# One core: the products of a gated state-space mixer written as eight term rows, all summed by TensorE's accumulating transposes, and the router's logits taken from a padded gate chunk

## The chip, the core and the metric

One core of one Trainium2 chip. Time is device microseconds for one execution of the whole program. The kernel before was run three times: 261.28, 262.47 and 263.16 us, median 262.47. TensorE is called PE in the rows, VectorE DVE, ScalarE ACT, GpSimd POOL and the DMA queue's own engine SP.

## The reference

Two residual layers over x of shape (16, 128, 256), all float32. The first is a mixer, the second a mixture of experts:

```python
# mixer: k = v = ctx (16, 128, 256) as 16 heads of 8 channels; q = layernorm(x)
kv  = einsum('bhil,bhjl->bijhl', k_, v_)              # products of channels in a head
y   = irfft(rfft(kv, 2L) * rfft(ssm_kernel, 2L))[..., :L]   # causal convolution, per head
out = y + kv * D                                       # skip
out = einsum('bijhl,bhil->bjhl', out, q_)              # sum over i
x   = x + tanh(g_xattn) * out
# experts: 2048 tokens of 256, E = 8 experts of capacity 256, hidden 352
xt = layernorm(x);  probs = softmax(xt @ Wg);  e = argmax(probs)
out = W2[e](silu(xt W1[e]) * (xt W3[e])) * gate, dropped past the capacity
shared = silu(xt @ sw1) * (xt @ sw3) @ sw2             # for every token
x = x + tanh(g_ffn) * (out + shared)
```

## The kernel before, in words

**Mixer.** The 16 batches go in 4 groups of 4. A group has 8 units of 2 heads. Time is cut in 2 blocks of 128; a causal convolution is then a matmul with a Toeplitz matrix (`toep`, the skip D added to it on VectorE by `add_skip`, L868 to L873). kv is symmetric in i and j, so a head has 36 planes of products. They are made a quarter of a group (4 heads) at a time by GpSimd (`kv_products`) and ScalarE (`squares`), for the next group while the present one runs. For a unit (`convolve`, L923) TensorE does per head one matmul of 144 and one of 288 columns into the PSUM buffer z[s % 2]. VectorE (`products`, `multiply`, L360 to L378) multiplies the 36 planes by q in five instructions, 1,024 elements a partition, into a buffer `prod` of eight term rows. GpSimd (`add_halves`, L503) adds rows 0 to 3 and 4 to 7 into four rows of `half`. When all 8 units of a group are done, `turn_r` (L956) transposes the four rows of each block and sums them in PSUM: 4 accumulating transposes for each of 8 blocks, 32 in all, in two parts k = 0 and 1. VectorE adds the result to x (`first_residual`).

**Norms and router.** Layernorm takes `norm_stats` on VectorE, `scale_and_bias` on GpSimd, `normalise` on ScalarE (`norm1` for q, `norm2` for the tokens), and a turn on TensorE (`turn_q`, `turn_xT`). Tokens and gate/up weights are split in a high and a low part (fp32r), and three products stand for one; `weights_high` (ScalarE) and `weights_low` (VectorE) split the weights, `xT_high` and `turned_low` the tokens. The router's logits are made by `logits` (L982): 4 batches x 2 x 3 matmuls of 8 columns. `choose` takes the argmax, `places` counts tokens per expert with two matmuls, `slot_of_token` and `gate` finish it, and GpSimd scatters the group's 512 token rows to HBM (`xd_scratch`) by indirect DMA.

**Experts.** 16 blocks of 256 tokens: 8 shared, 8 expert blocks. A block is three gate/up chunks (`gu`, 12 matmuls of 256 columns; the third chunk overlaps the second by 32 hidden columns, since 352 = 128 + 128 + 96) and a down product (`y`, 12 matmuls). Shared results are added to x and stored twice (output, and a base that experts gather from); an expert's rows are loaded back, turned (`turn_xe`), and its output is added to the gathered base and scattered. Five sets of expert weights are held; sets 0 and 1 have memory of their own, 2 to 4 lie in `half`.

**Order.** No planner: every engine runs the same loop over slots s, in which unit s is convolved and multiplied (s < 32), then chunk or down product number s - 17, then the steps that `STEPS` puts there: a step of group g is due at slot 8(g+1) + its number (for steps that prepare group g, 8(g-1) + its number). TensorE may be two units ahead of VectorE (two z buffers). All turns, logits and places share two PSUM banks `tp`, used in turn; the user of a bank waits until the reader of the one two before has finished (`tp_wait`, L286). After the loop comes the list of expert uses. All DMAs except the indirect ones are issued from one queue, SP, in program order.

## Time and profile before

| what | value |
|---|---|
| median of 3 runs | 262.47 us |
| profiled execution | 263.71 us |
| its span, first to last instruction | 261.9 us |
| mean granted TensorE clock | 0.924 |
| TensorE busy | 213.5 us (82%) |
| TensorE weight loads busy | 194.2 us |
| VectorE / ScalarE / GpSimd busy | 156.2 / 78.1 / 143.8 us |
| DMA | 31.82 MB, 121 GB/s over the span |

Busy times overlap, and matmuls are pipelined, so the price of a piece of TensorE work is read from the start of one piece to the start of the next. A row of the timeline gives start, duration, engine, line, operation, names and count, and in brackets how long the engine was idle before it and what released it. Waits of an engine matter only where a chain to the end passes through them.

### The profile page before, as it was taken

The numbers are of one execution on the slowest core, as the hardware profiler recorded it, in microseconds if no ns is written. First come the engines' busy times: TensorE is split into PE (matmuls) and PEld (weight loads), VectorE is DVE, ScalarE is ACT, GpSimd is POOL, SyncE is SP. The second block draws the span as 40 slices with busy tenths as digits, with TensorE's granted clock in tenths as the row PEclk, the third lists the DMA queues.
The fourth block names the chain that finished last, engine by engine and source line by source line (L and its number), as shares of the span: only waits on it lengthen the run. The fifth ranks groups of instructions, "written<-read, shape, count | busy, mean of one in ns | idle before, by whom it ended". The sixth has DMA issues, their size and how long they took to land. (4 is left out here: it accounts for less than half of the span.)

```text
span 261.9 us, 3970 instructions
## 1 busy us (share of the span) xinstructions
PE 213.5 (82%) x1360; PEld 194.2 (74%) x1360; DVE 156.2 (60%) x461; ACT 78.1 (30%) x146; POOL 143.8 (55%) x146
## 2 busy tenths in 40 slices
PE   0093987962999999999999969994798699999950
PEld 0061766841989989999899959993697699989940
DVE  5799577774389967867665352543255546665320
ACT  1080430481124254301343044330223333434100
POOL 1493999979718897353820640052004765756632
PEclk9998699999579999999997997799689999999995
DMA  7999603004500202021020467059004578843211
GB/s 163 342 377 370 240 0 123 0 1 140 192 1 1 83 0 83 0 99 66 0 80 3 144 205 225 0 161 292 25 4 137 161 233 252 264 124 97 77 54 40
DMA packets 23428, 31.82 MB, mean 121 GB/s; under 512 B 2750, under 2 KB 20902, under 8 KB 23408
## 3 DMA queue, kind: packets, MB, share of 16 engines
q1 hardware_dynamic: 21104, 25.52, 30.6%
q0 software_dynamic: 2304, 6.05, 7.0%
q8 instruction: 11, 0.18, 0.3%
q14 instruction: 9, 0.07, 0.1%
HBM read 21.30 MB, written 10.52 MB: 121 GB/s over the span
## 5 line engine op out<-in xcount | busy, mean ns | idle before, releaser
L368 DVE TENSOR_TENSOR prod<-z,qr 128x512 f32<-128x512 f32 (+4 forms) x160 | 47.3, 362 | 18.6 <-POOL half L510 15.3
L940 PE MATMUL z<-kv,toep 128*128 128x144 f32 x128 | 29.8, 318 | 22.8 <-DVE toep L872 12.8
L940 PEld LDWEIGHTS z<-kv,toep 128*128 128x128 f32 x128 | 24.6, 211 | 31.5 <-issue 26.1
L510 POOL TENSOR_TENSOR half<-prod 128x512 f32<-128x512 f32 x32 | 41.1, 1300 | 10.3 <-DVE prod L368 10.2
L943 PE MATMUL z<-kv,toep 128*128 128x288 f32 x128 | 46.1, 445 | 0.0
L549 POOL DMA_INDIRECT xd_scratch<-xrow,dest x16 | 17.4, 1088 | 32.7 <-DVE xrow L785 29.0
L564 POOL DMA_INDIRECT kv<-base_scratch,tok x16 | 19.6, 1222 | 25.5 <-issue 25.5
L1031 PE MATMUL fb<-xTh,wh_gu 128*128 128x256 f32 x100 | 32.8, 328 | 0.0
L349 POOL TENSOR_TENSOR kv<-ct 128x768 f32<-128x768 f32 x15 | 27.4, 1827 | 7.9 <-DMA ct<-ctxt 7.9
L1031 PE MATMUL z<-xTh,wh_gu 128*128 128x256 f32 x92 | 28.5, 310 | 1.5 <-issue 1.5
L1031 PE MATMUL fb<-xTh,wl_gu 128*128 128x256 f32 x100 | 29.3, 293 | 0.0
L1031 PE MATMUL fb<-xTl,wh_gu 128*128 128x256 f32 x100 | 29.3, 293 | 0.0
L1031 PE MATMUL z<-xTh,wl_gu 128*128 128x256 f32 x92 | 26.9, 292 | 0.0
L1031 PE MATMUL z<-xTl,wh_gu 128*128 128x256 f32 x92 | 26.9, 292 | 0.0
L575 POOL DMA_INDIRECT out<-kv,tok x16 | 17.1, 1070 | 17.0 <-DVE kv L823 12.8
L648 ACT ACTIVATE sg<-fb 128x256 f32<-128x256 f32 x25 | 9.6, 383 | 55.1 <-PE fb L1031 51.3
L648 ACT ACTIVATE sg<-z 128x256 f32<-128x256 f32 x23 | 8.7, 383 | 46.6 <-PE z L1031 44.6
L943 PEld LDWEIGHTS z<-kv,toep 128*128 128x128 f32 x128 | 22.3, 210 | 0.0
L1031 PEld LDWEIGHTS fb<-xTh,wh_gu 128*128 128x128 f32 x100 | 20.5, 205 | 0.7
L1031 PEld LDWEIGHTS fb<-xTh,wl_gu 128*128 128x128 f32 x100 | 20.4, 204 | 0.7
L1031 PEld LDWEIGHTS fb<-xTl,wh_gu 128*128 128x128 f32 x100 | 20.4, 204 | 0.0
L1031 PEld LDWEIGHTS z<-xTh,wh_gu 128*128 128x128 f32 x92 | 18.8, 205 | 1.8 <-issue 1.7
(103 smaller groups left out, 429.7 us busy)
## 6 DMA issues: line engine op xcount, KB each, us to landing
w_gu<-w SPq DMA_DIRECT2D x8, 352.0 KB
half<-w SPq DMA_DIRECT2D x8, 352.0 KB, 4.5
ct<-ctxt SPq DMA_DIRECT2D x3, 768.0 KB, 8.4
xd_scratch<-xrow SPq DMA_DIRECT2D x4, 516.0 KB, 9.7
kv<-xd_scratch SPq DMA_DIRECT2D x8, 258.0 KB
toep<-kpad SPq DMA_DIRECT2D x4, 512.0 KB, 7.5
x_sb<-x SPq DMA_DIRECT2D x4, 512.0 KB, 9.2
out<-x_sb SPq DMA_DIRECT2D x8, 256.0 KB
```

Source lines behind the costliest of these rows:

```text
L349: eng.tensor_tensor(dst, left, right, ALU.mult)
L368: return eng.tensor_tensor(view(prod, p0 + o, [[512, 2], *od]), view(src, zc + zo, [[stride, 2], *zd]), view(qr, q0 + qo, [[CW, 2], *qd]), ...
L510: pool.tensor_tensor(view(half, (g % 2) * H * 256 + 2 * u * 64, [[H * 64, TERMS], [64, 2], [1, 64]]), first, second, ALU.add).then_inc(hal ...
L549: pool.indirect_dma_start(out=xd, out_offset=bass.IndirectOffsetOnAxis(ap=dest[:, b:b + 1], axis=0), in_=xrow[:, g % 2, b % GB, :], in_off ...
L564: pool.indirect_dma_start(out=bg[:, e % BRING, t, :], out_offset=None, in_=base, in_offset=bass.IndirectOffsetOnAxis(ap=tok[:, e, t:t + 1] ...
L575: pool.indirect_dma_start(out=out_rows, out_offset=bass.IndirectOffsetOnAxis(ap=tok[:, e, t:t + 1], axis=0), in_=fin[:, e % 2, t, :], in_o ...
L648: act.activation(sg[:, k % SGS, :], bank[:, 0:256], ACT.Silu).then_inc(silu_done, 1)
L940: pe.matmul(view(z[s % 2], k * 512 + GB, [[PL, NPL], [1, GB]]), toep[:, h, P:2 * P], view(kv, o, [[PL, NPL], [1, GB]]), start=True, stop=F ...
L943: mm = pe.matmul(z[s % 2][:, k, 0:KVH], toep[:, h, 0:P], view(kv, o, [[1, KVH]]), start=False, stop=True, skip_group_check=True)
L1031: mm = pe.matmul(bank[:, m * 256:(m + 1) * 256], wt[w % 2][:, col:col + P], xt[:, place, k, first:first + 256], start=(k == 0 and j == 0), ...
```

## The change

1. `prod` and `half` are gone. `multiply` writes into one tensor `terms` of eight rows of 24 heads (a group uses 16 of them; odd groups start at head 8 and take their units in the order 4 to 7, 0 to 3, so that a group's second half may be written only when the group before has been turned). It takes six instructions in place of five, over the same 1,024 elements.
2. `add_halves` is gone from GpSimd. `turn_r` sums 8 rows for every block: 64 transposes a group, its two parts in slots of their own (`turn_r0`, `turn_r1`), and so are the two residual additions.
3. The router's weights are copied into the 32 spare columns of the shared weights' third chunk, now padded to 384 hidden columns. Chunk 2 of a shared block thus makes the logits; ScalarE copies 8 rows of them to `lgT`, and `logits` is 4 small transposes a group. Chunk 2 is run first of a block, at slots 8g + 16 and 8g + 17.
4. The steps are moved: ln2_apply is in slot 4 of a group's cycle (5 before), logits in 10 (7), scatter in 12 (10). Shared work fills the slots from 21 on, and all of it, y7 too, lies before the experts. The first skip additions are done four units ahead in place of all at the start.
5. All five expert weight sets lie in `terms`, and are loaded from the third shared store on. An expert's third chunk has 96 rows, not 128.
6. At the start x is loaded first, and the context for group 0 from ScalarE's queue. On GpSimd the kv products of a slot stand ahead of the scale.

The core of the diff:

```diff
+HP = 3 * 128
-F0_SLOT = 17
-LAG = 1
-PRODS = 2
-TERMS = 4
+SKIPS_AHEAD = 4
+REST_SLOT = 21
+TERMS = 8
+FULL_TERMS = 4
+HEADS = 24
+TROW = HEADS * 64
-EXPERT_SPLIT_SLOT = CONV + 12
+EXPERT_SPLIT_SLOT = CONV + 14
 STEPS = {
-    "ln1_stats": 0, "ln1_scale": 1, "ln1_apply": 2, "turn_q": 4,
-    "residual": 2, "ln2_stats": 3, "ln2_scale": 4, "ln2_apply": 5, "turn_xT": 6, "logits": 7,
-    "exp": 7, "places": 9, "gate": 9, "scatter": 10,
+    "ln1_stats": 1, "ln1_scale": 2, "ln1_apply": 2, "turn_q": 4,
+    "turn_r0": 1, "turn_r1": 2, "residual0": 2, "residual1": 3, "ln2_stats": 3, "ln2_scale": 4, "ln2_apply": 4,
+    "turn_xT": 6, "tokens_low": 7, "logits": 10, "exp": 10, "places": 11, "gate": 11, "scatter": 12,
 }
+def unit(s):
+    g, i = divmod(s, UNITS)
+    return g, (i + 4 * (g % 2)) % UNITS
+def first_head(g, u):
+    return 2 * u + 8 * (g % 2)
+def terms_of(g):
+    return TERMS if g < FULL_TERMS else TERMS // 2
+def shared_uses():
+    first = {8 * g + 16 + i: ("gu", 2 * g + i, 2) for g in range(NG) for i in range(2)}
+    rest = []
+    for g in range(NG):
+        m, n = 2 * g, 2 * g + 1
+        rest += [("gu", m, 0), ("gu", m, 1), ("gu", n, 0), ("y", m, 0), ("gu", n, 1), ("y", n, 0)]
...
-            mul(0, 0, 0, [[64, 4], [1, 64]], [[64, 4], [1, 64]], [[PL, 4], [1, 64]])
-            mul(256, 256, 32, [[32, 2], [1, 32]], [[0, 2], [1, 32]], [[32, 2], [1, 32]])
-            mul(320 + 8, 64, 0, [[72, 2], [1, 64]], [[64, 2], [1, 64]], [[0, 2], [1, 64]])
-            mul(448 + 24, 192, 0, [[1, 40]], [[1, 40]], [[1, 40]])
-            return mul(320, 192 + 40, 40, [[72, 3], [1, 8]], [[8, 3], [1, 8]], [[8, 3], [1, 8]])
+            mul(0, 0, 0, 0, [[TROW, 4], [1, 64]], [[64, 4], [1, 64]], [[PL, 4], [1, 64]])
+            mul(4, 0, 256, 32, [[32, 2], [1, 32]], [[0, 2], [1, 32]], [[32, 2], [1, 32]])
+            mul(5, 8, 64, 0, [[TROW + 8, 3], [1, 40]], [[64, 3], [1, 40]], [[0, 3], [1, 40]])
+            mul(7, 0, 192 + 40, 40, [[1, 24]], [[1, 24]], [[1, 24]])
+            mul(6, 0, 128 + 48, 48, [[48 - TROW, 2], [1, 16]], [[-72, 2], [1, 16]], [[-8, 2], [1, 16]])
+            return mul(5, 0, 64 + 56, 56, [[TROW + 56, 2], [1, 8]], [[48, 2], [1, 8]], [[-16, 2], [1, 8]])
...
             def load_expert(e):
                 if e == 0:
-                    sp.wait_ge(w_low_dve, 1)
-                    sp.wait_ge(w_low_pool, 1)
-                if e == 2:
                     sp.wait_ge(tp_ready, TP_AT[("r", NG - 1, 1)] + 1)
-                    sp.wait_ge(pool_consts, 7)
...
-            load_expert(0)
-            load_expert(1)
             for n in range(8):
...
+                if n == 2:
+                    load_expert(0)
+                    load_expert(1)
                 if 3 <= n < 6:
                     load_expert(n - 1)
...
-            def add_halves(s):
-                g, u = divmod(s, UNITS)
-                pool.wait_ge(prods, s + 1)
-                if g >= 2 and u == 0:
-                    pool.wait_ge(tp_ready, TP_AT[("r", g - 2, 1)] + 1)
-                o = (s % PRODS) * 1024
-                first, second = (view(prod, o + i * 256, [[64, TERMS], [512, 2], [1, 64]]) for i in range(2))
-                pool.tensor_tensor(view(half, (g % 2) * H * 256 + 2 * u * 64, [[H * 64, TERMS], [64, 2], [1, 64]]),
-                                   first, second, ALU.add).then_inc(halved, 1)
...
+                if blk < 8 and c == 2:
+                    if blk >= 2:
+                        act.wait_ge(tp_ready, TP_AT[("logits", blk // 2 - 1, 0)] + 1)
+                    act.activation(lgT[:, blk % 2 * 256:(blk % 2 + 1) * 256], bank[0:E, 0:256],
+                                   ACT.Copy).then_inc(lg_copied, 1)
...
             def products(s):
+                g, i = divmod(s, UNITS)
                 dve.wait_ge(z_ready, s + 1)
-                dve.wait_ge(q_done, s // UNITS + 1)
-                if s >= PRODS:
-                    dve.wait_ge(halved, s - PRODS + 1)
-                multiply(dve, s, z[s % 2], 0, 512).then_inc(prods, 1)
+                dve.wait_ge(q_done, g + 1)
+                before = g - 2 if i < 4 else g - 1
+                if before >= 0 and i % 4 == 0:
+                    dve.wait_ge(tp_ready, TP_AT[("r", before, 1)] + 1)
+                multiply(dve, s, z[s % 2]).then_inc(prods, 1)
...
-            def turn_r(g):
-                pe.wait_ge(halved, UNITS * (g + 1))
-                for k in range(2):
-                    n = TP_AT[("r", g, k)]
-                    tp_wait(pe, n)
-                    for j in range(2 * BLK):
-                        b, blk = 2 * k + j // BLK, j % BLK
-                        for t in range(TERMS):
...
+            def turn_r(g, k):
+                pe.wait_ge(prods, UNITS * (g + 1))
...
+                for j in range(2 * BLK):
+                    b, blk = 2 * k + j // BLK, j % BLK
+                    for t in range(terms_of(g)):
+                        src = view(terms, t * TROW + first_head(g, 0) * 64 + blk * GB + b, [[PL, CH]])
+                        mm = pe.matmul(tp[n % 2][:, j * P:(j + 1) * P], src, ident[:, :], is_transpose=True,
+                                       start=(t == 0), stop=(t == terms_of(g) - 1))
...
                 tp_wait(pe, n)
-                wait_xT(g)
-                if g == 0:
-                    pe.wait_ge(wg_low, 1)
+                pe.wait_ge(lg_copied, 2 * (g + 1))
                 for b in range(GB):
-                    for k in range(2):
-                        for j, (xt, wt) in enumerate(((xTh, wgh), (xTh, wgl), (xTl, wgh))):
-                            mm = pe.matmul(tp[n % 2][:, b * E:(b + 1) * E], xt[:, g % 2, k, b * P:(b + 1) * P],
-                                           wt[:, k, :], start=(k == 0 and j == 0), stop=(k == 1 and j == 2))
+                    mm = pe.transpose(tp[n % 2][:, b * E:(b + 1) * E], lgT[:, b * P:(b + 1) * P], ident[0:E, 0:E])
```

ScalarE's queue around slots 10 to 14, before. xn and xrow are normalised tokens for q and for the router, qr the copied q, wh_gu the high part of the shared weights:

```order
L587 ACTIVATE xn<-x_sb,nbias,rstd 128x256 [waits tp_ready,rstd_done]
L587 ACTIVATE xn<-x_sb,nbias,rstd 128x256 x3
L608 ACTIVATE kv<-ct 128x4x64 [waits z_ready,ctx_in2]
L617 ACTIVATE qr<-tp0 128x16x8x4 [waits tp_ready,prods]
L617 ACTIVATE qr<-tp1 128x16x8x4 [waits tp_ready]
L622 ACTIVATE qr<-qr 128x16x32 [waits tp_free_act]
L669 ACTIVATE wh_gu0<-w_gu 128x1408 [waits shared_gu_in]
L587 ACTIVATE xrow<-x_sb,nbias,rstd 128x256 [waits rstd_done]
L587 ACTIVATE xrow<-x_sb,nbias,rstd 128x256 x3
```

The same place in the changed kernel:

```order
L639 ACTIVATE xn<-x_sb,nbias,rstd 128x256 [waits tp_ready,rstd_done]
L639 ACTIVATE xn<-x_sb,nbias,rstd 128x256 x3
L660 ACTIVATE kv<-ct 128x4x64 [waits z_ready,ctx_in2]
L669 ACTIVATE qr<-tp0 128x16x8x4 [waits tp_ready,prods]
L669 ACTIVATE qr<-tp1 128x16x8x4 [waits tp_ready]
L674 ACTIVATE qr<-qr 128x16x32 [waits tp_free_act]
L639 ACTIVATE xrow<-x_sb,nbias,rstd 128x256 [waits rstd_done]
L639 ACTIVATE xrow<-x_sb,nbias,rstd 128x256 x3
L719 ACTIVATE wh_gu0<-shared_gu 128x1536 [waits router_placed,shared_gu_in]
```

The copy of the weights' high part has moved behind the normalisation of xrow.

TensorE at the end of slot 17 to slot 19, for group 1, in the changed kernel (tp0 and tp1 are the two shared banks):

```order
L1033 MATMUL tp0<-ident,terms 128x128 [waits tp_free_dve,prods]
L1033 MATMUL tp0<-ident,terms 128x128 x31
L1007 MATMUL z0<-kv,toep 128x36x4 [waits prods,kv_square,kv_pool]
L1010 MATMUL z0<-kv,toep 128x288
...
L1055 MATMUL tp1<-ident,lgT 128x8 [waits lg_copied,tp_free_dve]
L1055 MATMUL tp1<-ident,lgT 128x8 x3
L1033 MATMUL tp0<-ident,terms 128x128 [waits tp_free_dve,prods]
L1033 MATMUL tp0<-ident,terms 128x128 x31
```

(Left out is the convolution's second head, two rows like its first.) Before, the group's turn was one piece, in two banks:

```order
L965 MATMUL tp0<-ident,half 128x128 [waits tp_free_dve,halved]
L965 MATMUL tp0<-ident,half 128x128 x15
L965 MATMUL tp1<-ident,half 128x128 [waits tp_free_dve]
L965 MATMUL tp1<-ident,half 128x128 x15
L940 MATMUL z1<-kv,toep 128x36x4 [waits prods,kv_square,kv_pool]
L943 MATMUL z1<-kv,toep 128x288
```

The logits now lie between the two parts of the turn, and both parts use the same bank.

## Rows read from the trace of the kernel before

**Rows 1.** The page's costliest groups: xcount | busy, mean ns | idle before, releaser

```profile
L368 DVE TENSOR_TENSOR prod<-z,qr 128x512 f32<-128x512 f32 (+4 forms) x160 | 47.3, 362 | 18.6 <-POOL half L510 15.3
L510 POOL TENSOR_TENSOR half<-prod 128x512 f32<-128x512 f32 x32 | 41.1, 1300 | 10.3 <-DVE prod L368 10.2
```

**Rows 2.** Windows, all engines: length, busy of PE, PEld, DVE, ACT, POOL, clock, DMA

```profile
45.00:61.00 16.00, 13.57 (x89) 11.08 (x87) 11.48 (x40) 8.94 (x16) 13.69 (x14) 1.00 0.00 1
61.00:76.00 15.00, 10.50 (x42) 9.58 (x41) 7.89 (x29) 1.82 (x3) 9.68 (x9) 0.66 0.44 146
76.00:98.00 22.00, 22.00 (x159) 20.54 (x159) 19.00 (x62) 8.37 (x19) 18.13 (x19) 1.00 0.07 25
...
137.00:142.00 5.00, 5.00 (x31) 5.00 (x31) 2.22 (x11) 2.27 (x4) 0.00 (x0) 0.66 0.01 3
```

**Rows 3.** Timeline of TensorE, 12 to 71 us

```profile
12.76 0.82 PE L940 MATMUL z<-kv,toep 128*128 128x144 f32 x2 [12.76 <-DVE toep L872]
...
44.91 3.73 PE L965 MATMUL tp<-ident,half 128*128 128x128 f32 x32
48.47 0.41 PE L940 MATMUL z<-kv,toep 128*128 128x144 f32 x2
...
51.39 1.04 PE L953 MATMUL tp<-ident,xn 128*128 128x128 f32 x8
...
65.54 0.35 PE L991 MATMUL tp<-wgh,xTh 128*128 128x8 f32 x1 [4.50 <-DVE xTl L833]
...
70.66 0.83 PE L940 MATMUL z<-kv,toep 128*128 128x144 f32 x2
```

**Rows 4.** Timeline of TensorE, 87 to 169 us

```profile
87.20 0.41 PE L940 MATMUL z<-kv,toep 128*128 128x144 f32 x2
...
90.06 1.03 PE L953 MATMUL tp<-ident,xn 128*128 128x128 f32 x8
...
95.23 2.75 PE L1044 MATMUL fb<-w_d,hT 128*128 128x256 f32 x12
...
168.41 0.39 PE L1005 MATMUL tp<-acc,ones 128*128 128x32 f32 x2
```

**Rows 5.** Timeline of VectorE, 8 to 40 us

```profile
8.32 1.41 DVE L720 BATCH_NORM_STATS2 stats<-x_sb 128x6 f32<-128x256 f32 x4 [3.47 <-DMA x_sb<-x]
...
11.80 9.79 DVE L872 SCALAR_TENSOR_TENSOR toep<-anti,d_bc,toep 128x128 f32<-128x128 f32 x16
...
21.60 1.47 DVE L368 TENSOR_TENSOR prod<-z,qr 128x512 f32<-128x512 f32 x5
...
24.98 1.48 DVE L368 TENSOR_TENSOR prod<-z,qr 128x512 f32<-128x512 f32 x5
...
37.10 2.87 DVE L368 TENSOR_TENSOR prod<-z,qr 128x512 f32<-128x512 f32 x10 [1.24 <-POOL half L510]
```

**Rows 6.** Groups by form, two of the five multiplications of L368

```profile
L368 DVE TENSOR_TENSOR prod<-z,qr 128x512 f32<-128x512 f32 x32 | 22.0, 688 | 18.6 <-POOL half L510 15.3 <-PE z L943 3.3
...
L368 DVE TENSOR_TENSOR prod<-z,qr 128x48 f32<-128x48 f32 x32 | 6.3, 198 | 0.0
```

**Rows 7.** Timeline of ScalarE, 53 to 58 us

```profile
53.74 1.36 ACT L669 ACTIVATE wh_gu<-w_gu 128x1408 fp32r<-128x1408 f32 x1
55.70 2.08 ACT L587 ACTIVATE xrow<-x_sb,nbias,rstd 128x256 f32<-128x256 f32 x4 [0.60 <-POOL nbias L483]
```

**Rows 8.** Timeline of GpSimd, 172 to 200 us

```profile
172.18 1.04 POOL L549 DMA_INDIRECT xd_scratch<-xrow,dest  x1 [16.94 <-DVE xrow L785]
...
199.37 2.19 POOL L564 DMA_INDIRECT kv<-base_scratch,tok  x1 [20.96 <-issue]
```

**Rows 9.** Timeline of TensorE, 185 to 192 us

```profile
185.84 0.55 PE L1031 MATMUL z<-xTh,wh_gu 128*128 128x256 f32 x1 [1.46 <-issue]
...
191.10 0.84 PE L1054 MATMUL tp<-ident,kv 128*128 128x128 f32 x4
```

**Rows 10.** Waits: us in total, times, longest

```profile
PE tp L1054 <- DMA kv<-xd_scratch: 7.2, 3, 4.2
```

More of the change, by code:

```diff
@@ L104, in transposing_uses @@
     for s in range(SLOTS):
-        for what, step, parts in (("r", "residual", 2), ("q", "turn_q", 2), ("xT", "turn_xT", 2),
-                                  ("logits", "logits", 1), ("pos", "places", 1)):
+        for what, step, parts in (("logits", "logits", (0,)), ("r", "turn_r0", (0,)), ("r", "turn_r1", (1,)), ("q", "turn_q", (0, 1)),
+                                  ("xT", "turn_xT", (0, 1)), ("pos", "places", (0,))):
             if due(step, s) >= 0:
-                uses += [(what, due(step, s), k) for k in range(parts)]
+                uses += [(what, due(step, s), k) for k in parts]
     uses += [("xe", e, 0) for e in range(E)]
@@ L210, in build @@
         fin = after[:, o:o + 4 * L].rearrange("p (i t n) -> p i t n", i=2, t=2)
[L212 to L216 removed]
+        gu_set, down_set = [], []
+        for i in range(SETS):
             o = i * (GUW + DW)
[L218 to L219 removed]
+            gu_set.append(terms[:, o:o + GUW])
+            down_set.append(terms[:, o + GUW:o + GUW + DW])
         tok = sb("tok", [P, E, 2], I32)
@@ L1043, in feed_forward @@
                         for c in range(3):
-                            mm = pe.matmul(bank[:, t * L:(t + 1) * L], hT[:, blk % 2, c, t * P:(t + 1) * P],
-                                           down[:, c * L:(c + 1) * L], start=(c == 0), stop=(c == 2))
+                            mm = pe.matmul(bank[:, t * L:(t + 1) * L],
+                                           hidden(blk, c)[0:rows(blk, c), t * P:(t + 1) * P],
+                                           down[0:rows(blk, c), c * L:(c + 1) * L], start=(c == 0), stop=(c == 2))
                     mm.then_inc(f_ready, 1)
@@ L1063, in _ @@
                     convolve(s)
-                if s >= F0_SLOT:
-                    feed_forward(s - F0_SLOT)
-                for step, work in (("residual", turn_r), ("turn_q", turn_q), ("turn_xT", turn_xT),
-                                   ("logits", logits), ("places", places)):
+                if s in SHARED_AT:
+                    feed_forward(FU_AT[SHARED_AT[s]])
+                if due("logits", s) >= 0:
+                    logits(due("logits", s))
+                for k in range(2):
+                    if due(f"turn_r{k}", s) >= 0:
+                        turn_r(due(f"turn_r{k}", s), k)
+                for step, work in (("turn_q", turn_q), ("turn_xT", turn_xT), ("places", places)):
                     if due(step, s) >= 0:
```

323 lines of the change are left out of this document (176 added, 147 removed).

## The prediction

> **What bounds the kernel now.** I read the page first: TensorE is by far the busiest engine, so the question is when it is not busy, and when it is slow. The page's costliest groups show that VectorE's products wait 15.3 us for GpSimd's additions, 1.30 us each, 32 times [rows 1]; GpSimd's kv products stand between these. The windows by stage say where that matters [rows 2]: from 76:98 on TensorE hardly pauses; in 61:76 it is busy 10.5 of 15 us and its granted clock is 0.66; in 137:142 it is busy all the time and the clock is 0.66 again. TensorE's timeline gives the milestones [rows 3]: first convolution at 12.76; the first logits after a wait of 4.50, 24 matmuls of 8 columns; unit 16 at 70.66.
>
> **The milestones of the sum** are: unit 16 starts (70.7), the last places are done (168.8) [rows 3, 4], the first expert chunk starts (185.8), the end (261.9). Prices on TensorE at full clock, start to start: a unit's convolution 1.46 (two from 48.47 to 51.39), the old residual turn 3.56 for 32 transposes (44.91 to 48.47) [rows 3], a gate/up chunk 1.40 (87.20 to 90.06 is convolution and chunk), a down product 2.6 of its 2.75 [rows 4], turn_q and turn_xT 0.9 each (8 transposes at the 0.11 of those 32), the old logits 2.6 a group at full clock (24 loads of 128 columns at 0.11: the load sets the pace, not the 8 columns).
>
> **On TensorE alone the change is a loss.** Residual turns double: 4 x 3.6 = +14.3 us. Logits go: 5.1 (65.54 to 70.66, slow clock [rows 3]) + 3 x 2.6 = -12.9. Their 16 small transposes add about 4 x 0.45 = +1.8. Net +3.2, and for full-clock prices +5.7. So every gain must come from waits and clock.
>
> **Part 1, to unit 16.** VectorE's timeline [rows 5]: x group 0 lands at 8.3 (the stats waited 3.47 for it), all 16 skip additions run 11.80 to 21.5 at 0.61, and only then come the first products at 21.60. The change issues x first and the context from ScalarE's queue, so I let x land near 6.3; stats 2.0, own kv products 1.5, first two skips: first convolution at about 11 (12.76). Only 8 skips stand ahead of the first products, which then wait for q: 3.2 after the first turn_q starts at 14.2 (it follows a slow-clock convolution of 3.2), so 17.4 in place of 21.6. Up to the end of unit 7's products VectorE has 8 x 1.46 + 8 skips x 0.61 + stats 2.0 + 0.2 = 18.8; with a little slow-clock waiting that ends at 37 in place of 40.0 (two units from 37.10, 2.87). The 1.46: a unit is 1.40 now (21.60 to 24.98 less the stats of 2.0). It becomes six multiplications in place of five over the same 1,024 elements. By the forms of 512 and 48 elements, 688 and 198 ns [rows 6], one costs 147 ns fixed; five of 362 ns on average [rows 1] make 1.81 and take 1.40 to the next, so 82 of each overlap: +0.06. Bounds: 0, or 0.2 a unit (a whole small form), 6 us in all.
>
> Group 1 I walk by queue order, from products 7 = 0. TensorE: convolution 9, first turn (32 transposes) to 5.0, convolution 10, second turn to 10.1, convolution 11 to 11.5. VectorE: products 11 to 13.0, residual 0.7, stats to 15.7. GpSimd scale 1.3 (its kv products, now ahead of it in the slot, need only convolution 11 and are done by 13.8), ScalarE's normalisation 2.1: xrow at 19.1. Here a **new wait** appears. Today weights_high runs before that normalisation (53.74, then 55.70 [rows 7]); now ln2_apply is in slot 12 and comes first in ScalarE's order. So weights_high ends at 20.6, and VectorE, which has finished products 12 at 17.2, stands in weights_low(0) for 3.5 us; behind it are products 13 to 15, and convolutions 15 and 16 behind these. Convolution 16 starts at 24.5: 37 + 24.5 = 61.5, against 70.7. The 4.50 before the logits and their slow 5.1 are gone, and so is most of the waiting for GpSimd. **-9.2.**
>
> **Part 2, unit 16 to the last places.** Now 98.1. After: 16 convolutions 23.4, 20 chunks 28.0, 5 down products 13.0, six half turns of 32 transposes 21.4, turns of q and xT 3.5, the four small logits 1.8, four places of 0.36 (an estimate, their two records together) 1.4: 92.5. On top come the waits, from walking the slots in queue order as above. The first chunk waits 1.3 for tokens_low, a slot after turn_xT. In slots 18, 26 and 34 the order of banks is turn_r0, logits, turn_r1: turn_r1 takes the bank of turn_r0, and waits until products, residual0 (and in two the shared down addition) are through VectorE: 1.75, 1.0, 1.0. In slot 19 VectorE has products, residual, stats, places and gate, about 6.1 us, and turn_q in slot 20 needs the two banks that residual1 and places free: 0.3 and 2.0; in slot 27 the down products beside it cover that. The first router chunk of each later group waits for tokens_low: 0.7, 2.0, 2.0. Fourth normalisation 0.6, last one-hot 1.0, a down product 0.5. Together 14.2, so 106.7. The clock: at present this stretch loses about 8 to slow spells, among them those after the narrow logits bursts (137:142 [rows 2]: busy without a pause, clock 0.66). Those bursts leave; waits of 1 to 3 us come. I take 3. **106.7 + 3 - 98.1 = +11.6.**
>
> The Trainium skill, page "TensorE: Matmul & The Clock Gate", Part 1, says that the throttled state is the default and that activity releases it. The trace agrees where the engine had waited (61:76). What it would make of the new waits is the slower rival below; it changes no term here.
>
> **Part 3, places to the first expert chunk.** Now 17.0: scatter begins 3.4 after the places, and 13.7 later the chunk does (172.18 [rows 8], 185.84 [rows 9]). After, VectorE has nothing ahead of places and gate but one product of 0.4: 2.0. **-1.3.** TensorE has 13.4 of shared work left in this time, y7 now among it.
>
> **Part 4, the experts.** Now 76.1. y7's 2.6 is no longer in it. Three waits for rows sum to 7.2, the longest 4.2 ahead of the first expert [rows 10]; the other 3.0 come from queue order: rows 2 stand behind y7's store on the DMA queue, rows 3 behind the first expert's output, which waited for a gather at 199.37 that needs y7's store. With y7 before the experts both go. The first two chunks took 5.3 (185.84 to 191.10) against 2.8 at full clock, after waits of 4.2 and 1.46; one of 2.3 is left, for which I take 1.0 off (bounds 0 and 2.5). Expert weights: all are loaded after the last turn, from y2's store on, five sets before the first chunk as now; the first set has over 30 us. The 96-row third chunk streams the same 256 columns: nothing. Two more activation table loads lie on ScalarE between exp and silu, the least busy engine (8.4 of 22 us in 76:98): nothing. **-6.6.**
>
> **Sum**: -9.2 + 11.6 - 1.3 - 6.6 = -5.5. The span goes from 261.9 to 256.4; the profiled execution took 263.7, 1.2 over the median of 262.47. From the median: **257.0**.
>
> **Rivals.**
> (a) *Slower, the clock.* Part 2 now has seven waits where the stretch had one. A drop cost 2.5 us at 185.84. If five of them drop the clock, 12.5 in place of my 3: 266.5. It makes the kernel slower by 1% from the fifth drop on. For it: 61:76; against: in 45:61 TensorE was idle 2.4 of 16 us, in short waits, at full clock. Also by the page's rule, since each wait takes activity away. 0.15.
> (b) *Same: the early gain is handed back.* VectorE's queue is the pace in group 0 and 1; if x lands no sooner (8.3) and products cost 0.2 more a unit, 2 + 4 are lost: 263. 0.20.
> (c) *Faster: waits overlap.* From 76 to 98 VectorE was busy 19.0 of 22 and TensorE did not wait once [rows 2]. If half of my 14.2 is absorbed: 250. 0.18.
> (d) The forecast, -3 to -9: 0.47.
> That the change does not do what it says is excluded by its instruction order.
>
> The range 249 to 265 takes (b), (c), (d) and little of (a). 1%, 2.6 us, is what a measurement tells from nothing: faster 0.62 ((c) and nearly all of (d)), same 0.22, slower 0.16.
>
> **What would show it.** First convolution near 11; no wait of VectorE for GpSimd's additions; unit 16 at 59 to 64; a wait of 3 to 4 us before weights_low(0); in slot 18 a wait of the turn for residual0; the last places near 171; full clock after each group's logits; no wait for rows 2 and 3. The prediction is wrong if unit 16 starts after 66, if the stretch from there to the last places is over 115 or under 103, or if the expert part is not shorter than 72.

## The result, and the profile after

The changed kernel takes **264.23 us** (median of 20 executions, 262.07 to 267.05); the kernel before, beside it, 262.65 (20 executions, 260.95 to 264.15). Ratio 1.0082, interval 1.0045 to 1.0119. A second series gave 264.07 and a ratio of 1.014, interval 1.0075 to 1.0205. The forecast was 257.0 and faster. It is slightly slower: a change of 2 us, and a forecast that missed by 7. Ratios and their intervals are taken from the executions in the faster of the chip's two states alone, medians from all, so a ratio is not the quotient of two medians.

The parts of the program, by the milestones that the prediction used. The first profile (262.28 us, span 260.5, clock 0.986) is one of the shortest executions of this kernel; the second (263.60, span 261.9, clock 0.966) is nearer to its median.

| part | before | forecast | after, first profile | after, second profile |
|---|---|---|---|---|
| to unit 16 | 70.7 | 61.5 | 62.0 | 63.3 |
| unit 16 to the last places | 98.1 | 109.7 | 112.7 | 112.6 |
| places to the first expert chunk | 17.0 | 15.7 | 17.3 | 17.2 |
| from there to the end | 76.1 | 69.5 | 68.5 | 68.8 |
| span | 261.9 | 256.4 | 260.5 | 261.9 |

The page after. The first rows are its groups: VectorE's products, the first convolution matmuls with TensorE's waits for them, the residual turns.

```profile
L426 DVE TENSOR_TENSOR terms<-z,qr 128x512 f32<-128x512 f32 (+2 forms) x192 | 49.2, 327 | 21.5 <-PE z L1010 17.7
L1007 PE MATMUL z<-kv,toep 128*128 128x144 f32 x128 | 27.8, 299 | 22.3 <-DVE terms L426 12.1
...
L1033 PE MATMUL tp<-ident,terms 128*128 128x128 f32 x256 | 30.3, 277 | 4.5 <-DVE x_sb L803 4.5
```

Against [rows 1]: the 15.3 us that VectorE waited for GpSimd's additions are gone, but TensorE has finished unit 15 no sooner for it (62.0 for 61.0). VectorE's products even stand idle longer, 21.5 us for 18.6, only now behind TensorE, while TensorE waits 12.1 us for VectorE, and 4.5 before half turns. TensorE's waits, in total, times, longest:

```profile
PE z L1007 <- DVE terms L426: 12.1, 8, 3.0
...
PE fb L1094 <- issue: 6.5, 4, 2.2
PE tp L1033 <- DVE x_sb L803: 4.5, 3, 2.0
PE tp L1020 <- DVE t L854: 1.7, 1, 1.7
PE fb L1094 <- DVE xTl L894: 1.4, 1, 1.4
```

TensorE's timeline after, the places of the forecast:

```profile
10.18 0.82 PE L1007 MATMUL z<-kv,toep 128*128 128x144 f32 x2 [10.18 <-DVE toep L935]
...
38.36 3.74 PE L1033 MATMUL tp<-ident,terms 128*128 128x128 f32 x32
...
60.47 0.48 PE L1007 MATMUL z<-kv,toep 128*128 128x144 f32 x2 [2.82 <-DVE terms L426]
...
62.00 0.41 PE L1007 MATMUL z<-kv,toep 128*128 128x144 f32 x2
...
65.00 0.38 PE L1094 MATMUL fb<-xTh,wh_gu 128*128 128x256 f32 x1 [1.38 <-DVE xTl L894]
...
77.00 3.82 PE L1033 MATMUL tp<-ident,terms 128*128 128x128 f32 x32 [2.05 <-DVE x_sb L803]
...
87.08 0.66 PE L1020 MATMUL tp<-ident,xn 128*128 128x128 f32 x4 [1.73 <-DVE t L854]
...
135.96 0.36 PE L1094 MATMUL fb<-xTh,wh_gu 128*128 128x256 f32 x1 [2.17 <-issue]
...
174.31 0.39 PE L1068 MATMUL tp<-acc,ones 128*128 128x32 f32 x2
...
192.03 0.36 PE L1094 MATMUL fb<-xTh,wh_gu 128*128 128x256 f32 x1 [1.46 <-issue]
```

Nearly every wait that was walked out stands there with its size. The largest new one, on VectorE, and the two ScalarE rows that cause it (ScalarE first):

```profile
54.43 2.08 ACT L639 ACTIVATE xrow<-x_sb,nbias,rstd 128x256 f32<-128x256 f32 x4 [1.52 <-POOL nbias L544]
56.41 1.47 ACT L719 ACTIVATE wh_gu<-shared_gu 128x1536 fp32r<-128x1536 f32 x1
```

```profile
52.94 1.54 DVE L426 TENSOR_TENSOR terms<-z,qr 128x512 f32<-128x512 f32 x6
57.91 0.96 DVE L907 TENSOR_TENSOR wl_gu<-shared_gu,wh_gu 128x768 fp32r<-128x768 f32 x1 [3.43 <-ACT wh_gu L719]
58.78 3.00 DVE L426 TENSOR_TENSOR terms<-z,qr 128x512 f32<-128x512 f32 x12
```

3.43 us, forecast 3.5: the weights' high part comes behind the normalisation, VectorE stands in the weights' low part, and two units' products stand behind it. The same windows as in [rows 2], where these overlap:

```profile
61.00:76.00 15.00, 12.58 (x90) 10.96 (x88) 10.47 (x42) 4.85 (x11) 7.37 (x8) 1.00 0.01 2
76.00:98.00 22.00, 18.73 (x135) 17.05 (x136) 15.45 (x67) 9.95 (x19) 9.94 (x11) 1.00 0.07 25
...
137.00:142.00 5.00, 5.00 (x33) 5.00 (x32) 0.85 (x2) 2.13 (x5) 0.00 (x0) 0.66 0.01 3
```

61:76 is at full clock now, in this profile. But in 76:98 TensorE is busy 18.7 us where it was 22.0: the stretch that never paused now has gaps. And 137:142 still shows 0.66 with TensorE busy throughout. Here no burst of logits stands ahead of it; a wait of 2.17 us ended 1.1 us before the clock fell.

### The profile page after: what moved, and what is told of

Read it like the earlier page. It is cut to its first block, busy times and chain, and to the rows that moved or that the text cites. A ratio compares the mean times of both kernels' runs of the same rounds, so it can differ in the third digit from the quotient of the medians.

```text
span 260.5 us, 4071 instructions
## 1 busy us (share of the span) xinstructions
PE 208.4 (80%) x1408; PEld 186.8 (72%) x1408; DVE 154.0 (59%) x494; ACT 82.2 (32%) x155; POOL 103.5 (40%) x111
## 4 chain that ended last, share of the span: by engine, by line
PE 60%; DVE 17%; issue 9%; DMA 5%; ACT 4%; POOL 2%; POOLq 1%; DVEq 0%; ACTq 0%; SPq 0%
PE fb L1094 13%; PE tp L1033 10%; PE z L1094 9%; PE z L1010 8%; PE fb L1108 6%; PE z L1108 6%; DVE terms L426 6%; PE z L1007 4%; DVE stats L779 3%; DVE toep L935 3%; DMA x_sb<-x 2%; DVE x_sb L803 2%; DMA xd_scratch<-xrow,dest 2%; PE tp L1119 1%; DMA kv<-xd_scratch 1%
## 5 line engine op out<-in xcount | busy, mean ns | idle before, releaser
L426 DVE TENSOR_TENSOR terms<-z,qr 128x512 f32<-128x512 f32 (+2 forms) x192 | 49.2, 327 | 21.5 <-PE z L1010 17.7
L1007 PE MATMUL z<-kv,toep 128*128 128x144 f32 x128 | 27.8, 299 | 22.3 <-DVE terms L426 12.1
L1094 PE MATMUL fb<-xTh,wh_gu 128*128 128x256 f32 (+1 forms) x104 | 32.8, 315 | 7.9 <-issue 6.5
L1033 PE MATMUL tp<-ident,terms 128*128 128x128 f32 x256 | 30.3, 277 | 4.5 <-DVE x_sb L803 4.5
L1033 PEld LDWEIGHTS tp<-ident,terms 128*128 128x128 f32 x256 | 29.6, 194 | 4.9 <-issue 2.6
L1094 PE MATMUL fb<-xTh,wl_gu 128*128 128x256 f32 (+1 forms) x104 | 29.7, 285 | 0.0
L1094 PE MATMUL fb<-xTl,wh_gu 128*128 128x256 f32 (+1 forms) x104 | 29.7, 285 | 0.0
L1094 PE MATMUL z<-xTh,wh_gu 128*128 128x256 f32 (+1 forms) x88 | 25.9, 295 | 1.2 <-DVE xTl L901 1.2
L1094 PE MATMUL z<-xTl,wh_gu 128*128 128x256 f32 (+1 forms) x88 | 24.4, 278 | 0.0
L1094 PE MATMUL z<-xTh,wl_gu 128*128 128x256 f32 (+1 forms) x88 | 24.4, 278 | 0.0
L601 POOL DMA_INDIRECT xd_scratch<-xrow,dest x16 | 16.0, 999 | 19.7 <-DVE xrow L845 16.0
L1094 PEld LDWEIGHTS fb<-xTl,wh_gu 128*128 128x128 f32 (+1 forms) x104 | 20.0, 192 | 0.0
```

The source lines that it names most:

```text
L426: return eng.tensor_tensor(view(terms, t0 + row * TROW + col, [[64, 2], *td]), view(src, zo, [[512, 2], *zd]), view(qr, q0 + qo, [[CW, 2], ...
L601: pool.indirect_dma_start(out=xd, out_offset=bass.IndirectOffsetOnAxis(ap=dest[:, b:b + 1], axis=0), in_=xrow[:, g % 2, b % GB, :], in_off ...
L1007: pe.matmul(view(z[s % 2], k * 512 + GB, [[PL, NPL], [1, GB]]), toep[:, h, P:2 * P], view(kv, o, [[PL, NPL], [1, GB]]), start=True, stop=F ...
L1033: mm = pe.matmul(tp[n % 2][:, j * P:(j + 1) * P], src, ident[:, :], is_transpose=True, start=(t == 0), stop=(t == terms_of(g) - 1))
L1094: mm = pe.matmul(bank[0:rows(blk, c), m * 256:(m + 1) * 256], wt[w % 2][:, col:col + rows(blk, c)], xt[:, place, k, first:first + 256], st ...
```

## The experiments

Theory A: the loss is made of TensorE's doubled turns and of waits at hand-overs that the queue orders make, each of them on the path. Rivals: the clock takes what is gained; the waits hide one another; VectorE or GpSimd is the pace. All are edits of the changed kernel; each ratio is to the kernel before, run beside it. The table gives profile milestones in us. "Waits" are TensorE's bracketed waits in the second part.

| kernel | ratio to before [interval] | median | unit 16 | second part (waits) | third | fourth | span |
|---|---|---|---|---|---|---|---|
| changed, again | 1.014 [1.0075, 1.0205] | 264.07 | 63.3 | 112.6 (15.7) | 17.2 | 68.8 | 261.9 |
| all groups folded | 0.974 [0.970, 0.979] | 256.06 | 63.6 | 105.2 (14.4) | 17.3 | 68.6 | 254.6 |
| groups 2 and 3 folded | 0.972 [0.967, 0.977] | 257.16 | 63.2 | 105.5 (15.7) | 17.1 | 68.9 | 254.8 |
| tokens_low in slot 6 | 0.977 [0.973, 0.982] | 256.16 | 61.9 | 105.9 (9.4) | 17.4 | 68.6 | 253.7 |
| weights_high(0) first | 0.997 [0.993, 1.000] | 261.80 | 60.6 | 112.8 (15.6) | 17.4 | 69.5 | 260.2 |
| logits in slot 9 | 0.996 [0.990, 1.001] | 261.78 | 63.2 | 112.0 (10.9) | 18.1 | 68.6 | 261.9 |
| rows ahead of y6's store | 1.007 [1.002, 1.012] | 263.29 | 63.3 | 112.7 (15.6) | 16.9 | 69.0 | 261.8 |
| eight skips ahead | 1.010 [1.005, 1.016] | 267.09 | 64.7 | 112.9 (14.4) | 17.1 | 68.5 | 263.1 |
| old start of transfers | 1.018 [1.010, 1.026] | 266.02 | 63.7 | 112.8 (14.3) | 17.4 | 69.0 | 262.9 |
| four order edits | 0.945 [0.941, 0.949] | 249.68 | 59.9 | 101.3 (6.1) | 17.7 | 68.5 | 247.5 |
| four edits and folding | 0.911 [0.907, 0.915] | 241.45 | 61.7 | 92.1 (6.9) | 17.7 | 68.5 | 240.0 |

The kernel before had medians of 262.5 to 264.9 in the series that these ran in: the ratios are to be compared, not the medians.

### Folding: what the doubled turns cost

GpSimd adds rows 4 to 7 of a unit to rows 0 to 3, in place, and a group is turned with 32 transposes again.

```diff
-FULL_TERMS = 4
+FULL_TERMS = 0
```

> The changed kernel with one number altered: GpSimd folds rows 4 to 7 into rows 0 to 3 for all four groups (32 additions of 128x512), and TensorE turns 4 rows, 32 transposes a group in place of 64. Everything else of the change stays. Theory A (TensorE is the pace from unit 16 on, so each doubled turn costs its full length): three turns of the dense stretch get 3.6 us shorter each, -10.7, less up to 1.5 a group for the wait for the last fold; the stretch from unit 16 to the last places, 112.7 in the changed kernel, becomes 103 to 107, and the time 6 to 9 us shorter than the changed kernel's, ratio to before 0.975 to 0.985. Theory B (VectorE's chains of residual, norm, router are the pace, the turns lie beside them): under 3 us gained, ratio 0.997 to 1.008.

256.06 us, ratio 0.974. The second part is 7.4 shorter than in the second profile of the changed kernel, unit 16 no sooner. Then only groups 2 and 3 were folded:

```diff
-FULL_TERMS = 4
+FULL_TERMS = 2
```

> The changed kernel with FULL_TERMS 2: groups 0 and 1 keep eight rows and 64 transposes, groups 2 and 3 are folded by GpSimd and have 32. Theory A: in groups 2 and 3 TensorE is the bound and GpSimd idle, so the whole 2 x 3.7 us of transposes come off, 256.8, and most of the 8.1 that folding all groups gave (the other two groups, where VectorE's queue is the pace, give little). Rival B, the gain lies evenly over the groups: 260.2. Rival C, it lies in the first groups, where fewer transposes let group 1 start sooner: 262 or more.

257.16, ratio 0.972, the same gain. So nearly all of what was measured lies in the two late groups: 64 transposes less, 0.112 us each (3.59 for 32 in the half turn from 69.40 to 72.99 of the changed kernel), 7.2 us; the second part is 7.0 shorter. Here are the turns of this second kernel, against 256 transposes and 30.3 us in the changed one:

```profile
L1033 PE MATMUL tp<-ident,terms 128*128 128x128 f32 x192 | 23.1, 277 | 4.6 <-DVE x_sb L803 4.6
```

In group 0 fewer transposes only lengthen waits, and unit 16 is no sooner. Group 1's saving is another case: the profile of the kernel with all groups folded has it, and loses it again to the clock. Its turn of q is 1.8 us ahead of the changed kernel's second profile (86.61 for 88.37), and the first router chunk of the next group only 0.1 ahead (100.59 for 100.66). Between the two a unit runs at slow clock, first here with all groups folded, then in the changed kernel:

```profile
86.61 1.01 PE L1020 MATMUL tp<-ident,xn 128*128 128x128 f32 x4 [1.73 <-DVE t L854]
87.42 0.69 PE L1007 MATMUL z<-kv,toep 128*128 128x144 f32 x2
```

```profile
88.37 0.66 PE L1020 MATMUL tp<-ident,xn 128*128 128x128 f32 x4 [1.73 <-DVE t L854]
88.86 0.41 PE L1007 MATMUL z<-kv,toep 128*128 128x144 f32 x2
```

The half turn at 76.98 is slow there too, 3.21 us for 16 transposes. Other executions of this kernel had a mean clock of up to 0.966 for this one's 0.939, and spans at most 1.6 us shorter, so group 1 may be worth up to that; no run here separates it.

### The hand-overs, one at a time

**tokens_low** in the slot of turn_xT, so that the first router chunk of a group doesn't wait a slot for the low part:

```diff
-    "turn_xT": 6, "tokens_low": 7,
+    "turn_xT": 6, "tokens_low": 6,
```

> The changed kernel with tokens_low in the slot of turn_xT (6) in place of the one after it. Theory A (the waits of 1.4, 0.7, 2.2 and 2.2 us before the first router chunk of each group are for tokens_low, one slot late in VectorE's order): they go, apart from some 0.5 in VectorE's wait for ScalarE's high part; 3 to 5 us less, ratio 0.989 to 0.997. Theory B (VectorE now stands waiting for ScalarE in slot 6 and its products come later): under 1.5 us, ratio 1.002 to 1.010.

256.16, ratio 0.977: more than was expected. TensorE's waits in this kernel:

```profile
PE tp L1033 <- DVE x_sb L803: 4.6, 3, 2.0
PE fb L1094 <- issue: 1.8, 2, 1.5
```

Of 6.5 us in four waits of the chunks ahead of which nothing is named, 1.8 are left, and the 1.4 for xTl has gone too; half turns wait as before. The waits of the second part fall by 6.3 and the part by 6.7: no wait behind them took their place. Unit 16 also starts 1.4 us sooner, which brings the gain to 8. That part is not shown to belong to the edit: it arises on VectorE at 17.7, before the first slot that was edited, where two skip additions take 0.60 us for 2.32 in the changed kernel's second profile.

**weights_high(0)** ahead of the normalisation on ScalarE, as before the change:

```diff
+                if s == SPLIT_SLOT:
+                    weights_high(0)
                 if due("ln2_apply", s) >= 0:
                     norm2(due("ln2_apply", s))
...
-                if s == SPLIT_SLOT:
-                    weights_high(0)
```

> The changed kernel with ScalarE's split of the shared weights put ahead of the normalisation of xrow in slot 12, its old place. Theory A (the wait of 3.4 us of VectorE for the weights is on the path to unit 16): the wait of 2.8 us of TensorE before units 15 and 16 (60.5) goes, unit 16 starts 2 to 2.8 earlier (59.5 in place of 62.0), and the time falls by as much: ratio to before 0.998 to 1.001. Theory B (the next chain, xrow to tokens_low to the first router chunk, ends as late): the first router chunk starts within 0.7 of its 65.0, and nothing is gained, ratio 1.005 to 1.010.

261.80, ratio 0.997. Unit 16 starts at 60.6 for 63.3: unit 15 starts 1.3 sooner (59.01 for 60.31), behind a wait of 0.94 for 2.82, and takes 1.5 less, since the clock did not fall (see the second profile below).

**Logits one slot sooner**, so that the banks of both half turns are free:

```diff
-    "logits": 10, "exp": 10,
+    "logits": 9, "exp": 9,
```

> The changed kernel with logits, choose and exp one slot earlier (9 in place of 10), so that the logits' bank lies ahead of both halves of the turn and no half takes the bank of the other. Theory A (the waits of 2.05, 1.25 and 1.25 us of the second half turn for residual0 are on the path): these three waits go, a wait of some 0.5 for ScalarE's copy of the logits comes in each group, and the wait of 1.0 for the last one-hot goes too: 3 to 4.5 us less, ratio 0.991 to 0.997. Theory B: the waits move on to the next user of a bank (turn_q, places) or to VectorE's longer slot 17; under 1 us, ratio 1.004 to 1.010.

261.78, ratio 0.996. The three waits of half turns (4.6) are gone, but four of 0.55 for the copied logits come, and the third part has two new waits, 0.61 for hidden values and 0.69 for the first expert's rows (18.1 for 17.2). In the profile, one of its longer executions (263.59), the second part is only 0.6 shorter at 4.8 us less waiting: the clock was low in two stretches more, and took most of the gain back. By the ratio the edit gains 1.2% (of 1.0082) or 1.8% (of 1.014).

**The rows' loads** ahead of y6's store on the DMA queue:

```diff
+                if n == 6:
+                    for e in range(2):
+                        load_rows(sp, e)
                 sp.wait_ge(f_free, FU_AT[("y", n, 0)] + 1)
...
-                if n == 6:
-                    for e in range(2):
-                        load_rows(sp, e)
```

> The changed kernel with the row loads of experts 0 and 1 ahead of y6's store on the DMA queue. Theory A: the rows were held 1.1 us behind that store (it starts at 185.16, the rows at 186.31, the turn at 189.95), so the first expert chunk comes 1 to 1.5 us sooner and the time is 262.7 to 263.2, ratio 1.002 to 1.004. Rival B: the row loads wait for the scatter's completion, and y6's output is stored later, so the experts' gathers wait in their turn: 264 or more.

263.29, ratio 1.007, which the measurement cannot tell from the changed kernel's 1.008 and 1.014. The third part is 0.4 us shorter, where theory A had 1 to 1.5. The queue in the changed kernel's second profile, and then with the edit:

```profile
186.49 0.38 SPq L512 DMA_DIRECT2D out<-x_sb  x1
186.91 0.47 SPq L512 DMA_DIRECT2D base_scratch<-x_sb  x1
188.05 0.90 SPq L394 DMA_DIRECT2D kv<-xd_scratch  x2
```

```profile
187.96 0.88 SPq L394 DMA_DIRECT2D kv<-xd_scratch  x2
188.88 0.47 SPq L515 DMA_DIRECT2D out<-x_sb  x1
```

The loads start at 187.96 instead of 188.05, though nothing stands before them: they wait for the scatter to land, whose last part is issued at 182.5. And the turn of the rows begins right behind y7's product on TensorE in both. So the store cost 0.1 us on the queue, and at most 0.4 in the part.

### The start

All skip additions ahead of the first products again, as before the change:

```diff
-SKIPS_AHEAD = 4
+SKIPS_AHEAD = 8
```

> The changed kernel with SKIPS_AHEAD 8 in place of 4: all 16 skip additions stand ahead of the first products again, as before the change. Eight of them at 0.61 us move from between products to ahead of them; the first products wait for q until 16.2 in any case, and eight skips from 10 us on end at 15, sixteen at 20. Theory A, VectorE's queue is the pace to unit 7, and its total work stays: products 7 end at most 1 us later, the time is 264 to 265. Rival B, the skip order is what brought the early gain of the first part (first products at 16.2 for 21.6): unit 16 is 3 to 4 us later, 267 to 268.

267.09 beside 264.87, ratio 1.010, within the interval of the changed kernel's own. In the profile TensorE stands 8.87 us before unit 2, at slow clock afterwards:

```profile
24.39 0.82 PE L1007 MATMUL z<-kv,toep 128*128 128x144 f32 x2 [8.87 <-DVE terms L426]
```

The first products come 6.5 later (22.7 for 16.2 on VectorE); at the first turn, behind unit 7's products, and at unit 15 2.7 of this is left, at unit 16 only 1.4 and at the end 1.2. The last step is the clock's: here it falls one unit later than in the changed kernel, at unit 16, and the slow spell takes the place of the wait of 1.38 for xTl.

```profile
63.00 0.48 PE L1007 MATMUL z<-kv,toep 128*128 128x144 f32 x2 [2.82 <-DVE terms L426]
...
64.70 0.69 PE L1007 MATMUL z<-kv,toep 128*128 128x144 f32 x2
```

So neither theory holds as it stands: A's "at most 1 us" behind unit 7 was 2.7, and B's 3 to 4 at unit 16 did not come. The median alone would read as B's 267, but the kernel before is 2.2 us longer in this series too, and the profiled execution is the shortest of six. The transfers in their old order:

```diff
-            load_x(0)
-            sp.dma_start(d_bc[:, :], ...)
+            sp.dma_start(ct[:, 0, 0:4 * CW], ctxt[0, :, 0:4 * CW]).then_inc(ctx_first, 16)
             load_toeplitz(0)
+            load_x(0)
+            sp.dma_start(d_bc[:, :], ...)
+            sp.dma_start(ct[:, 0, 4 * CW:], ctxt[0, :, 4 * CW:]).then_inc(ctx_in[0], 16)
...
-            act.dma_start(ct[:, 0, 0:4 * CW], ctxt[0, :, 0:4 * CW]).then_inc(ctx_first, 16)
-            act.dma_start(ct[:, 0, 4 * CW:], ctxt[0, :, 4 * CW:]).then_inc(ctx_in[0], 16)
```

> The changed kernel with the old start of the transfers: the context of group 0, then the first Toeplitz rows, then x, all from the one DMA queue, nothing from ScalarE's queue. Theory A, the start brought the first convolution forward by 2.6 us and everything behind it in VectorE's queue: with the old start x lands at 8.3 for 6.1, the first products come 2.2 later, unit 16 at 64 for 62, and the time is 2 us longer, 266.3. Rival B, VectorE has slack between the first products and unit 16, and the time is 264 to 265. Rival C, the skip order makes the start without effect, since Toeplitz rows landing earlier take back what x loses: under 264.

266.02, ratio 1.018 against 1.014 beside it, which the measurement cannot tell apart. The first convolution is at 12.4 for 9.9, unit 16 at 63.7 for 63.3, the end at 262.9 for 261.9. The profile speaks for slack (B), the median for something up to 2 us; between these it stays open. Either way, 2.5 us at the start are worth a small part of it.

### The changed kernel a second time

Without an edit:

> The changed kernel itself once more, word for word, for a second profile and for its ratio to the kernel before beside the kernels of this series. Its first 20 executions lay between 262.1 and 267.1 us. Theory A: the spread is TensorE's granted clock, which differs from one execution to the next (spans of 260.4 at a clock of 0.986, of 264.8 at 0.959); the ratio to the kernel before is 1.008 again, and if the profiled execution is a long one, its clock row shows one or two stretches of reduced clock more than the first profile, each behind a wait, while all milestones between them stand. Rival B: the difference lies in waits for transfers, which then differ in length between the two profiles.

264.07, ratio 1.014. The profiled execution has clock 0.966, and it shows where, in two stretches more than the first profile (theory A). Windows with the same columns as [rows 2], of this second profile, then of the first:

```profile
20.00:30.00 10.00, 6.65 (x25) 5.03 (x26) 9.93 (x35) 2.72 (x6) 5.58 (x6) 0.66 0.98 365
58.00:66.00 8.00, 4.62 (x16) 3.53 (x16) 6.11 (x21) 0.98 (x3) 6.78 (x5) 0.79 0.00 1
135.00:145.00 10.00, 7.83 (x55) 7.78 (x55) 2.71 (x8) 2.94 (x6) 0.00 (x0) 0.83 0.01 2
```

```profile
20.00:30.00 10.00, 4.60 (x25) 3.33 (x26) 9.93 (x34) 3.59 (x8) 5.83 (x7) 1.00 0.99 367
58.00:66.00 8.00, 4.16 (x24) 3.34 (x25) 7.57 (x25) 1.14 (x3) 6.91 (x5) 1.00 0.00 1
```

In 58:66 the fall costs 1.5 us, unit 15 at half speed behind the 2.82 us for the weights' low part:

```profile
60.31 0.82 PE L1007 MATMUL z<-kv,toep 128*128 128x144 f32 x2 [2.82 <-DVE terms L426]
...
63.31 0.41 PE L1007 MATMUL z<-kv,toep 128*128 128x144 f32 x2
```

3.00 us for the unit (60.31 to 63.31) against 1.53 in the first profile (60.47 to 62.00), behind the same wait. The Trainium skill, page "TensorE: Matmul & The Clock Gate", Part 1, has the throttled state as the default, left by activity; these rows agree. In 137:142 it is less plain: in the kernel before, TensorE was busy 14.00 of the 14 us from 128 to 142, and the clock fell in the midst of them, at 137.0. Nine of the twelve profiles have the 2.82 us wait before unit 15 in full, and eight of these have the low stretch behind it, all but the very first (one of the eight a unit later); the three kernels with the weights first have none. In 20:30 the slow clock costs nothing: VectorE is busy 9.93 of 10 us in both, and the first turn starts at 38.22 here and at 38.36 there.

### All order edits together, and with folding

The four order edits of above in one kernel, still with eight rows:

> The changed kernel with four edits of order together, and the eight term rows kept: weights_high(0) ahead of norm2 in slot 12, logits and exp in slot 9 instead of 10 (so both halves of a turn have banks free), tokens_low in slot 6 instead of 7, and the row loads of experts 0 and 1 ahead of y6's store on the DMA queue. Each alone gave, against the changed kernel's 264.2: 261.8, 261.8, 256.2, and the last was not run alone (1.5 us by the profile). Theory A, the loss is waits at hand-overs in queue order, each on the path by itself: the four add, 264.2 - 2.4 - 2.4 - 8.0 - 1.5 = 249.9. Rival B, the waits are shared (with one gone VectorE or ScalarE is late at the next place), so that tokens_low's gain holds most of the others: 253 to 256. Rival C, the clock takes back what is saved: over 256. Under A the logits' move leaves waits of 0.6 before each group of logits and no wait of a half turn for x_sb.

249.68, ratio 0.945: theory A to 0.3 us, in part by luck. Its sum took 1.5 for the rows' loads, which alone gave nothing that can be told from noise, and the kernel before took 264.87 in this series for 262.65 in the first. What stands is that the edits add up and do not share their gain. Its waits:

```profile
PE tp L1055 <- ACT lgT L703: 2.2, 4, 0.6
PE fb L1094 <- issue: 1.8, 2, 1.5
PE tp L1020 <- DVE t L854: 1.7, 1, 1.7
```

Against the second profile of the changed kernel, unit 16 is 3.4 sooner and the second part 11.3 shorter; the third is 0.5 longer. Its page has this clock row, full everywhere but at the end, with no edit that is about the clock:

```profile
PEclk9999999999999999999999999999999999999996
```

Then the same with FULL_TERMS = 0:

> The same four edits of order and in addition GpSimd folds rows 4 to 7 of every unit into rows 0 to 3 (FULL_TERMS 0), so a turn is 32 transposes again. Folding alone gave 256.1 for 264.2, that is 8.1 of the 15 us that 128 transposes cost. Theory A, doubled transposes are a cost of TensorE's path independent of the order: 249.9 - 8 = 242. Rival B, with the waits out of the way VectorE and GpSimd (1.29 us a fold, beside kv products of 1.8) become the pace, and folding gives only half: 246. Rival C, it gives nothing or costs, since a half turn then waits for the last fold of its group: 250 or more. Under A there are under 8 us of waits of VectorE's products for GpSimd.

**241.45 us, ratio 0.911, interval 0.907 to 0.915**: the best kernel of the study, 8.9% below the kernel before and, by the two ratios, 9.6% below the changed one. GpSimd's folds have the size of the old additions, 1.3 us, 32 times [rows 1]:

```profile
L568 POOL TENSOR_TENSOR terms<-terms 128x512 f32<-128x512 f32 x32 | 41.4, 1308 | 13.8 <-DVE terms L426 13.6
```

but VectorE's products have no wait for one: with rows for every unit of a group instead of two `prod` buffers nothing is held up behind a late fold but the group's turn. The second part gains 9.2 (three groups' turns at 3.6 would be 10.8), the first loses 1.8. The first turn starts after a wait of 2.70 that the trace gives no name; I take it for the group's last fold, since the first of two folds that begin at 40.47 ends at about 41.7, and the turn starts at 41.84. The clock is slow behind that wait: 16 transposes have a row of 3.35 us, for 1.95 in the next half turn. Group 1's saving, which the clock had taken in the single edit's profile, counts here.

## Why the prediction was wrong

**The mechanism held in the main, the sum did not.** Three steps failed, all to the same side: "92.5" of TensorE work in part 2 measured 95.6; the clock behind the new wait of part 1, counted at nothing, cost 1.5; and the third part, 15.7 as a scatter's chain, measured 17.2. The waits of part 2, 14.2 in the forecast, were 15.6. The terms against the second profile: part 1 +1.8, part 2 +2.9, part 3 +1.5, part 4 -0.7; together 5.5, the whole of the forecast gain. The remaining 1.7 of the 7.2 is the base: the profile of before lies 1.1 above its median of 262.65, that of after 0.6 below the 264.2, and the forecast carried the gap of before's over unchanged.

*Part 1, -9.2 forecast, -7.4 to -8.7 measured.* x landed at 6.1 (forecast 6.3), the first convolution at 10.2 and 9.9 (11), the first turn at 38.4, the wait for the weights' low part 3.43 (3.5), unit 16 at 62.0. The products of a unit take 1.46 with six instructions, as forecast. What failed is the clock after the new wait, counted at nothing: 1.5 us in the usual execution. And the words about the gain were off. Before, TensorE had finished unit 15 at 61.04 (65.54 less the wait of 4.50 [rows 3]); now that happens at 62.0 or 63.3. The gain is the logits that no longer stand ahead of unit 16, 9.6 us, less 1.0 to 2.3. The sooner start and skip order are worth 0.4 and 1.4 at unit 16 by the experiments (0.4 and 2.7 at unit 15), and the new wait of 2.82 eats them.

*Part 2, +11.6 forecast, +14.5 and +14.6 measured.* The step that failed most is "92.5" of TensorE work. The waits were forecast at 14.2 and are 15.6; half turns 2.05, 1.25, 1.25 for 1.75, 1.0, 1.0; router chunks 0.71, 2.17, 2.18 for 0.7, 2.0, 2.0; the turn of q 0.54 and 1.73 for 0.3 and 2.0. The clock cost 1.5 for 3. But the work, starts to starts less the waits and the slow piece, is 95.6: convolutions and chunks 53.6 for 51.4, turns 21.8 for 21.4, the rest 20.2 for 19.7. A price from pieces in unbroken work is too low for a piece that stands next to a wait, on either side: unit 16 takes 1.62 to the wait behind it for 1.46, the chunk at 65.00, first behind that wait, 1.52 for 1.40. With twelve waits this could make most of the 2.2. The clock term was right in sign: the mean granted clock of the part is 0.98, before 0.92. But the fall in 137:142, which the forecast tied to the logits' bursts, is still there without one.

*Part 3, -1.3 forecast, +0.2 measured.* Two chains end close together, and both were priced too low. The scatter starts 2.8 after the places for 2.0, and the first expert chunk 14.5 behind it for 13.7; in the first profile the profile's own chain runs that way, through 4.92 us from the last scatter to the loads and 3.51 of loading. In the second profile it runs through TensorE's own work, "13.4 of shared work": 14.2 by its rows, and a wait of 0.98 besides for the hidden values before y7's product, then 2.1 for the turn and the tokens. That makes 17.2. (With the logits in slot 9 the turn waits 0.69 for the rows, so the first chain isn't far behind.) The store ahead of the loads, which looked like the cause, is cleared by experiment.

*Part 4, -6.6 forecast, -7.3 to -7.6 measured.* Of the waits for rows [rows 10] none over 0.4 us is left.

**The rivals.** (a), the clock, fell, though the waits were twelve, not its seven: the mean rose from 0.924 to 0.966 and 0.986, and a wait of 1 to 2 us in part 2 was mostly followed by full clock; the drops behind the waits of 2.82 and 2.17 us cost 1.5 each. In single executions of the variants it took more (logits in slot 9, all groups folded). (c) fell: the waits were not absorbed; with the four order edits the second part has 9.6 us of waits less and is 11.3 shorter. (b) is nearest in its time of 263, not in its cause: x did land sooner and products cost what they should.

Shown by experiment: the doubled turns cost 7 to 8 us, of which 7 in groups 2 and 3; the tokens' low part a slot too late 6.7 in its own part, 8 by the median; the weights' order and the logits' slot 1 to 2% each by ratio; the four order edits together 14.4 of span. With the slots mended the same eight rows are a gain of 5.5%: the change lost more in the table of slots than in the rows, whose price was forecast. Only argued: that slower pieces next to a wait explain the 2.2 us, and what the last fold has to do with the wait of 2.70. Why the clock is low in 137:142 stays open.

## What to carry to other kernels

Taking a wait from a busy engine's feeder gains nothing where that engine then waits for the next hand-over: walk the queues slot by slot, and before building the change mend every slot in which a consumer comes first, since those waits together were here worth their full length. Price a walk with waits in it from pieces that stand next to waits; here most of the small errors had one sign. An addition moved to an idle engine is good where its consumer has a whole group's time, and bad where only two buffers lie between: it was the two buffers, not GpSimd's 1.3 us, that made VectorE wait in the kernel before, since folds of the same length and number hold up none of its products.

## What the runs showed of the hardware

- The same program differs by 5 us from one execution to the next, together with TensorE's clock: 20 executions of the changed kernel have spans of 260.3 to 265.3 at mean clocks of 0.986 to 0.959. The kernel with the four order edits, which waits less, lay within 2 us in its six: 249.06 to 250.91, at 0.979 to 0.992.
- The clock is 0.66 in 137:142 in both kernels with TensorE busy 5.00 of 5 us, both doing chunks of 256 columns. In the kernel before, 24 logits matmuls of 8 columns end at 137.0, where the clock falls, and TensorE had not paused since 128. In the changed kernel a chunk that had waited 2.17 us began at 135.96, and the clock fell at about 137.1. The order edit of tokens_low, which takes that wait away, has no low stretch there (nor has the kernel with the weights first, which keeps the wait). What it hangs on stays open.
- An accumulating transpose of 128 x 128 float32 costs TensorE 0.112 us in a row of 32, start to start (69.40 to 72.99).
